# Last group's scatters in one row ahead of all stores, no fills behind the stores, and two more root batches on VectorE

## The chip, the cores and the metric

The kernel runs on one core of one Trainium2 chip. The metric is the device time of one execution in microseconds (us); lower is better. The engines are TensorE (PE), ScalarE (ACT), VectorE (DVE), GpSimd (POOL) and SyncE (SP), which issues plain DMAs. GpSimd issues the indirect DMAs.

## The reference

The input is x, 4 x 1024 rows of 128 float32. Two stages follow each other, each with a residual and a layer norm.

```python
x = _layernorm(x + _L0_attn_ref(x, ...), axis=-1)    # linear attention, 16 heads of 8, 32 features each
x = _layernorm(x + _L0_ffn_ref(x, ...), axis=-1)
# _layernorm: (x - mean) / sqrt(var + 1e-05)
# _L0_ffn_ref:
scores = jnp.einsum('bsh,he->bse', x, wr) + br
expert_id = jnp.argmax(scores, axis=-1)
h = jax.nn.gelu(jnp.einsum('bsh,ehf->ebsf', x, w1) + b1[:, None, None, :], approximate=False)
y = jnp.einsum('ebsf,efh->ebsh', h, w2) + b2[:, None, None, :]
out = jnp.einsum('ebsh,bse->bsh', y, one_hot)        # every row keeps the one of 8 experts that it chose
```

## The kernel before, in words

**Attention.** The 4096 rows are 32 tiles of 128 rows, in 8 groups of four (G = 8, GT = 4). Keys and values come first, then, group by group, queries, attention, output projection, residual and layer norm. ScalarE writes the normalised rows of a group into `x1`, and VectorE works out for each row its expert and its row number `dest` in a DRAM buffer `sorted_rows` in which the rows lie by expert.

**Scatter.** `scatter(g, tiles)` on GpSimd writes tiles of 128 rows of group g to their places in `sorted_rows`, one indirect DMA each (the issuing line is L553). Each row takes its token number along.

**Experts.** NT = 39 tiles of 128 sorted rows run through the FFN of their expert, tile t in step t. SP loads the rows of a tile (`load_rows`) and its first weight (`load_weights`). A sorted tile may be loaded only once the rows in it have been scattered: tiles 0 to 8 wait for groups 0 to 3, tiles 9 to 16 for groups 0 to 5, and tiles from NB = 17 on for all eight groups (L456). On TensorE, step s transposes tile s + 2 (L821), multiplies tile s + 1 by the first weight (`up`, L828), and tile s by the second (`down`, L841). ScalarE applies GELU (L1004). `down(t)` needs the output bank of tile t - 4, so `add_row(t - 4)` must be done.

**VectorE's step.** `tile_step(s)` adds the product of tile s to its rows (`add_row`, L1334), adds the bias of tile s + 1 (`add_bias`, L1328), takes mean and variance of tile s (L1338, L1342), and normalises the tiles that the table `NORMALISED_IN` lists for step s (`normalise_tile`, L1378). For the normalisation it needs 1/sqrt(var + eps), and that comes in one of three ways. Tiles in `BATCHES` get it from a power on GpSimd (`inverse_deviations`, L570), for which VectorE first adds epsilon (`add_row_epsilon`, L1348). Tiles in `ROOTS` get it from 12 small VectorE instructions (`root`, L1359 to L1369): a first guess from the bits of the number and three Newton steps, four instructions in each of the three steps after the last tile of the batch. Tiles 37 and 38 get it from ScalarE's logarithm and exponential and three VectorE instructions (L1622 to L1633).

**Store.** `store(t)` on GpSimd waits until tile t is normalised and writes its rows to the output by token number, one indirect DMA (L581). SP waits for all 39 stores at the end.

**GpSimd's order** is written out by hand. It takes its queue in program order. Behind the scatters of the last three groups and behind the stores of tiles 0 to 31 stands `keep_apart()`: a fill of `apart`, 128 x 408 float32, that nothing reads (L576), and that waits for the fill before it. `POWER_BEFORE` says ahead of which store a power stands. At the end of the attention part the order is:

```python
scatter(G - 2, range(GT))
inverse_deviations(0)
for t in range(GT):
    scatter(G - 1, (t,))
    store(t)
for t in range(GT, NT):
    if t in POWER_BEFORE:
        inverse_deviations(POWER_BEFORE[t])
    store(t)
```

Of the kernel before, what the change touches and what calls it, by code (L numbers as in the profile page):

```python
# [22 lines left out]
I32 = mybir.dt.int32  # L23
# [10 lines left out]
def build(nc, x, w_qkv, proj, w_out, b_out, wr, br, w1, b1, w2, b2, out):  # L34
# [24 lines left out]
    with ctx:  # L59
# [290 lines left out]
        def rank_slots(g):  # L350
# [10 lines left out]
        BATCHES = [range(0, 6), range(22, 25), range(25, 28), range(28, 31), range(31, 33), range(33, 35), range(35, 37)]  # L361
        ROOTS = [range(t, t + 4) for t in range(6, 22, 4)]
# [9 lines left out]
        NORMALISED_IN = {s: (s - 6,) for s in range(6, 25)}  # L372
        NORMALISED_IN |= {25: (19, 20), 26: (21, 22), 27: (23,), 28: (24,), 29: (25, 26), 30: (27,), 32: (28, 29), 33: (30,), 34: (31, 32),
                          36: (33, 34)}
        POWER_BEFORE = {19: 1, 24: 2, 28: 3, 29: 4, 32: 5, 34: 6}
# [90 lines left out]
        def _(pool):  # L466
# [78 lines left out]
            def scatter(g, tiles):  # L545
                ring = g % XR
                pool.wait_ge(dest_ready, g + 1)
                pool.wait_ge(number_ready, g + 1)
                if g == 0:
                    pool.wait_ge(prefilled, 16 * NPF)  # L550
                for i in tiles:
                    pool.wait_ge(x1_ready, GT * g + i + 1)
                    g_.indirect_dma_start(out=sorted_rows, out_offset=bass.IndirectOffsetOnAxis(ap=dest[:, ring, i:i + 1], axis=0),  # L553
                                          in_=x1[:, ring, i, :], in_offset=None).then_inc(scattered[ring], 16)
                    if g >= G - 3:
                        keep_apart()
# [22 lines left out]
            def store(t):  # L579
                pool.wait_ge(y_ready, t + 1)  # L580
                g_.indirect_dma_start(out=out_rows, out_offset=bass.IndirectOffsetOnAxis(ap=row_slot(t)[:, D:D + 1].bitcast(I32), axis=0),  # L581
                                      in_=row_slot(t)[:, 0:D], in_offset=None, bounds_check=last_token,
                                      oob_is_err=False).then_inc(stored, 16)
                if t < 32:
                    keep_apart()
# [30 lines left out]
            for t in range(GT):  # L616
                scatter(G - 1, (t,))
                store(t)
            for t in range(GT, NT):
                if t in POWER_BEFORE:  # L620
                    inverse_deviations(POWER_BEFORE[t])
                store(t)
# [425 lines left out]
        def _(dve):  # L1048
# [301 lines left out]
            def root(n, i):  # L1350

                at = slice(ROOTS[n][0], ROOTS[n][-1] + 1)
                first = guess[:, 0, :]
                now = guess[:, (i - 3) // 3 % 2, :]
                better = guess[:, ((i - 3) // 3 + 1) % 2, :] if i < ROOT_STEPS - 1 else rstd3[:, at]
# [4 lines left out]
                elif i == 1:  # L1360
                    op = v.tensor_scalar(bits_half[:, :], ve3[:, at].bitcast(I32), 1, None, ALU.arith_shift_right)
                elif i == 2:
                    op = v.tensor_scalar(first.bitcast(I32), bits_half[:, :], -1.0, float(0x5F3759DF), ALU.mult, ALU.add)
                elif i % 3 == 0:
                    op = v.tensor_tensor(var_guess[:, :], ve3[:, at], now, ALU.mult)
                elif i % 3 == 1:
                    op = v.scalar_tensor_tensor(less_half[:, :], var_guess[:, :], -0.5, now, ALU.mult, ALU.mult)
                else:
                    op = v.scalar_tensor_tensor(better, less_half[:, :], 1.5, now, ALU.add, ALU.mult)  # L1369
# [272 lines left out]
            add_row(NT - 2)  # L1642
            add_bias(NT - 1)
            row_statistics(NT - 2)
            row_moments(NT - 2)
            normalise_tile(last[0])
            normalise_tile(last[1])
            add_row(NT - 1)
# [38 lines left out]
```

## Time and profile before

| | |
|---|---|
| device time, median of 3 runs | 221.98 us (221.76 to 222.09) |
| profiled execution, its own time | 221.01 us |
| profiled execution, span from first to last instruction | 219.3 us |
| TensorE busy | 194.5 us (89% of the span), mean granted clock 0.964 |
| VectorE busy | 161.8 us (74%) |
| ScalarE busy | 145.4 us (66%) |
| GpSimd busy | 142.1 us (65%) |

The shares are means over the span. The attention part takes the first 120 us or so; the expert tiles run from there to the end. The rows further below are read from the trace of the same execution. A row of a timeline gives the start in us, the duration in us, the engine, the line, the operation and, in brackets, the idle time of the engine ahead of it and what ended it.

### The profile page before, as it was taken

Reading aid. Unit: us, or ns where it says so; the run is one execution under the profiler, and the core shown is the slowest. Engines: PE = TensorE matmul, PEld = TensorE weight load, DVE = VectorE, ACT = ScalarE, POOL = GpSimd, SP = SyncE. Lnnn points to the kernel's source line nnn. Section 1 sums busy time; section 2 is a strip of 40 time slices with the busy share of each in tenths; the row PEclk is TensorE's granted clock in tenths of the full one; section 3 lists DMA queues with packets and bytes.
Section 4 is the critical chain, followed back from the end, with each engine's and each line's share of the span. In section 5 each row is a group of like instructions: output and inputs, shape, how many; then the busy total and the mean of one; then the engine's idle time right before and its main releaser. Section 6 shows DMA issues by size and latency. Waiting matters only on the chain.

```text
span 219.3 us, 6084 instructions
## 1 busy us (share of the span) xinstructions
PE 194.5 (89%) x1698; PEld 154.7 (71%) x1698; DVE 161.8 (74%) x607; ACT 145.4 (66%) x379; POOL 142.1 (65%) x202
## 2 busy tenths in 40 slices
PE   7999999999999999999998989999499999999300
PEld 2677888888764565545443979899399999999200
DVE  2477778786755999999999768798938788375561
ACT  3487788888757677787675488785346666666420
POOL 8425142342599024676653787988987879988985
PEclk9999999999999999999999999999969999999855
DMA  4899999999993000110117673786378775750010
GB/s 110 230 369 417 411 408 402 401 400 397 304 273 83 0 1 1 52 37 25 40 52 240 176 217 109 196 232 183 92 229 229 225 210 182 203 149 24 26 36 7
DMA packets 28417, 40.46 MB, mean 184 GB/s; under 512 B 3497, under 2 KB 18126, under 8 KB 28384
## 3 DMA queue, kind: packets, MB, share of 16 engines
q1 hardware_dynamic: 26112, 35.80, 51.2%
q0 software_dynamic: 2272, 4.27, 5.7%
q8 instruction: 15, 0.25, 0.5%
q14 instruction: 18, 0.15, 0.2%
HBM read 17.95 MB, written 22.56 MB: 185 GB/s over the span
## 4 chain that ended last, share of the span: by engine, by line
PE 58%; POOL 21%; DVE 6%; issue 5%; ACT 3%; DMA 3%; another core or an unknown queue 1%; SPq 0%; DVEq 0%; ACTq 0%; POOLq 0%
PE pair L319 19%; POOL out_dram L581 11%; PE bank L675 6%; PE pair L828 6%; POOL apart L576 5%; PE pair L841 4%; PE bank L755 4%; PE pair L778 3%; POOL sorted_rows L553 3%; PE pair L755 3%; POOL rstd L570 3%; PE pair L720 2%; PE pair L645 2%; PE bank L655 2%; PE bank L319 2%
## 5 line engine op out<-in xcount | busy, mean ns | idle before, releaser
L1004 ACT ACTIVATE qfeat<-pair,w_sb 128x128 f32<-128x128 f32 x156 | 44.6, 368 | 21.8 <-issue 11.3
L828 PE MATMUL pair<-xsT,w_slot 128*128 128x128 f32 x312 | 42.3, 280 | 0.6 <-issue 0.2
L553 POOL DMA_INDIRECT sorted_rows<-x,dest x32 | 32.0, 1001 | 13.6 <-issue 6.5
L828 PEld LDWEIGHTS pair<-xsT,w_slot 128*128 128x128 f32 x312 | 38.6, 195 | 1.5 <-issue 1.3
L592 POOL TENSOR_TENSOR ksum<-kfeat 128x512 f32<-128x512 f32 x12 | 16.6, 1380 | 31.1 <-DVE kfeat L1092 31.1
L319 PE MATMUL pair<-wkv_part,xT_all 128*128 128x256 f32 x192 | 34.1, 321 | 1.5 <-ACT vals L927 0.8
L841 PE MATMUL pair<-w_sb,qfeat 128*128 x232 | 31.7, 281 | 0.5 <-DVE res L1149 0.5
L319 PEld LDWEIGHTS pair<-wkv_part,xT_all 128*128 128x128 f32 x192 | 28.5, 188 | 5.0 <-issue 4.9
L581 POOL DMA_INDIRECT out_dram<-x_all x26 | 26.0, 999 | 6.9 <-issue 4.3
L841 PEld LDWEIGHTS pair<-w_sb,qfeat 128*128 128x128 f32 x232 | 29.0, 196 | 0.8 <-issue 0.7
L319 PE MATMUL pair<-xT_all,wq_part 128*128 128x512 f32 x72 | 24.2, 456 | 0.0
L940 ACT ACTIVATE qexp<-pair,minus_one 128x512 f32<-128x512 f32 x24 | 16.5, 688 | 10.2 <-PE pair L319 10.1
L576 POOL MEMSET apart<- 128x408 f32 x44 | 20.8, 472 | 0.0
L1092 DVE SCALAR_TENSOR_TENSOR kfeat<-pair,qexp 128x512 f32<-128x512 f32 x16 | 11.0, 691 | 11.2 <-ACT vals L927 7.5
L534 POOL TENSOR_TENSOR rstd<-var_eps,minus_half 128x4 f32<-128x4 f32 x8 | 8.4, 1049 | 16.3 <-DVE var_eps L1168 16.2
L1121 DVE SCALAR_TENSOR_TENSOR qfeat<-pair,qexp 128x512 f32<-128x512 f32 x24 | 16.3, 683 | 2.4 <-ACT qexp L940 2.3
L1378 DVE TENSOR_SCALAR x_all<-x_all,mv,rstd 128x128 f32<-128x128 f32 x24 | 9.0, 437 | 9.8 <-POOL rstd L570 9.7
L581 POOL DMA_INDIRECT out_dram<-xs x13 | 13.0, 1000 | 3.1 <-issue 1.8
L319 PEld LDWEIGHTS pair<-xT_all,wq_part 128*128 128x128 f32 x72 | 13.9, 193 | 1.6
L994 ACT COPY xsT<-pair 128x128 f32<-128x128 f32 x39 | 10.8, 277 | 6.3 <-PE pair L821 2.7
L917 ACT ACTIVATE qexp<-pair,zero 128x512 f32<-128x512 f32 x16 | 11.0, 689 | 5.0 <-PE pair L319 3.8
L973 ACT ACTIVATE x<-res,shift,rstd 128x128 f32<-128x128 f32 x32 | 14.0, 491 | 0.1
(203 smaller groups left out, 418.4 us busy)
## 6 DMA issues: line engine op xcount, KB each, us to landing
sorted_rows<-pad_rows SPq DMA_DIRECT2D x11, 1584.0 KB, 22.4
w_slot<-in_L_ffn_w_dram SPq DMA_DIRECT2D x39, 256.0 KB
x_all<-in_L_attn_x_dram SPq DMA_DIRECT2D x8, 256.0 KB, 5.0
w_sb<-in_L_ffn_w_dram SPq DMA_DIRECT2D x4, 512.0 KB, 13.8
x_all<-sorted_rows SPq DMA_DIRECT2D x26, 66.0 KB
xs<-sorted_rows SPq DMA_DIRECT2D x13, 66.0 KB
w_sb<-in_L_ffn_b_dram SPq DMA_DIRECT2D x1, 512.0 KB, 7.0
sorted_rows<-x,dest POOLq DMA_INDIRECT x32
```

Source lines behind the costliest of these rows:

```text
L319: last = nc.tensor.matmul(out[:, to], weights[:, w, :], moving[:, m, of], start=(start and w + m == 0), stop=(w == 1))
L553: g_.indirect_dma_start(out=sorted_rows, out_offset=bass.IndirectOffsetOnAxis(ap=dest[:, ring, i:i + 1], axis=0), in_=x1[:, ring, i, :], i ...
L576: g_.memset(apart[:, :], 0.0).then_inc(apart_set, 1)
L581: g_.indirect_dma_start(out=out_rows, out_offset=bass.IndirectOffsetOnAxis(ap=row_slot(t)[:, D:D + 1].bitcast(I32), axis=0), in_=row_slot( ...
L592: g_.tensor_tensor(ksum[:, n % 2, :], kfeat[:, at, :], kfeat[:, at + 1, :], ALU.add).then_inc(ksum_ready, 1)
L755: last = mm(out[heads, :], kv_diag[:, at:at + CD], qfeat[:, g % 2, k, :], start=True, stop=True, skip_group_check=True)
L828: last = mm(h_bank[t % 2][:, k * P:(k + 1) * P], w1_slot[:, t % WB, k * P:(k + 1) * P], xsT[:, t % 2, :], start=True, stop=True)
L841: last = mm(y_bank[t % 4][:, 0:D], hT[:, t % 2, k * P:(k + 1) * P], w2_sb[:, bass.ds(w_at[t] + k * D, D)], start=(k == 0), stop=(k == FC - 1))
L940: a_.activation(qexp[:, (n + 2) % QB, :], q_bank[n % QB][:, :], ACT.Exp, bias=minus_one[:, :]).then_inc(q_exp, 1)
L973: a_.activation(x1[:, g % XR, i, 0:D], res[:, par, i, :], ACT.Identity, bias=shift[:, par, i:i + 1], scale=rstd[:, par, i:i + 1]).then_inc ...
L1004: a_.activation(hT[:, t % 2, k * P:(k + 1) * P], h_bank[t % 2][:, k * P:(k + 1) * P], ACT.Gelu, bias=w2_sb[:, bass.ds(w_at[t] + (FF + D + ...
L1121: v.scalar_tensor_tensor(qfeat[:, g % 2, k, :], q_bank[n % QB][:, :], 1.0, qexp[:, (n + 2) % QB, :], ALU.max, ALU.min).then_inc(q_done, 1)
```

## The change

Five things change.

1. The four scatters of group 7 stand one behind the other, ahead of store 0. Before, store 0 stood behind the first scatter, store 1 behind the second, and so on.
2. No store has a fill behind it (32 fills fewer). Of groups 5 and 6 the last scatter has none either (2 fewer). The scatters of group 7 keep theirs.
3. Tiles 22 to 28 move from GpSimd powers to VectorE roots, as batches 22 to 25 and 26 to 28. `root` works on as many columns as its batch has tiles.
4. Tiles 29 to 36 are powers in three batches (29 to 31, 32 and 33, 34 to 36), ahead of stores 27, 30 and 34. With batch 0 to 5 that makes four powers in the expert part where there were seven.
5. `NORMALISED_IN` follows, and in the step of tile 37 tile 34 is normalised ahead of `add_bias(38)`, tiles 35 and 36 behind the moments of tile 37.

```diff
-        BATCHES = [range(0, 6), range(22, 25), range(25, 28), range(28, 31), range(31, 33), range(33, 35), range(35, 37)]
-        ROOTS = [range(t, t + 4) for t in range(6, 22, 4)]
+        BATCHES = [range(0, 6), range(29, 32), range(32, 34), range(34, 37)]
+        ROOTS = [range(t, t + 4) for t in range(6, 26, 4)] + [range(26, 29)]
...
-        NORMALISED_IN = {s: (s - 6,) for s in range(6, 25)}
-        NORMALISED_IN |= {25: (19, 20), 26: (21, 22), 27: (23,), 28: (24,), 29: (25, 26), 30: (27,), 32: (28, 29), 33: (30,), 34: (31, 32),
-                          36: (33, 34)}
-        POWER_BEFORE = {19: 1, 24: 2, 28: 3, 29: 4, 32: 5, 34: 6}
+        NORMALISED_IN = {s: (s - 6,) for s in range(6, 28)}
+        NORMALISED_IN |= {28: (22, 23), 29: (24,), 30: (25,), 31: (26,), 32: (27, 28), 33: (29, 30), 34: (31,), 35: (32, 33)}
+        POWER_BEFORE = {27: 1, 30: 2, 34: 3}
...
-                    if g >= G - 3:
+                    if g >= G - 3 and (i < GT - 1 or g == G - 1):
                         keep_apart()
...
                                       oob_is_err=False).then_inc(stored, 16)
-                if t < 32:
-                    keep_apart()
...
             inverse_deviations(0)
-            for t in range(GT):
-                scatter(G - 1, (t,))
-                store(t)
-            for t in range(GT, NT):
+            scatter(G - 1, range(GT))
+            for t in range(NT):
                 if t in POWER_BEFORE:
                     inverse_deviations(POWER_BEFORE[t])
                 store(t)
...
             def root(n, i):
-
+                count = len(ROOTS[n])
                 at = slice(ROOTS[n][0], ROOTS[n][-1] + 1)
-                first = guess[:, 0, :]
-                now = guess[:, (i - 3) // 3 % 2, :]
-                better = guess[:, ((i - 3) // 3 + 1) % 2, :] if i < ROOT_STEPS - 1 else rstd3[:, at]
+                first = guess[:, 0, 0:count]
+                now = guess[:, (i - 3) // 3 % 2, 0:count]
+                better = guess[:, ((i - 3) // 3 + 1) % 2, 0:count] if i < ROOT_STEPS - 1 else rstd3[:, at]
...
             last = BATCHES[-1]
             add_row(NT - 2)
+            normalise_tile(last[0])
             add_bias(NT - 1)
             row_statistics(NT - 2)
             row_moments(NT - 2)
-            normalise_tile(last[0])
             normalise_tile(last[1])
+            normalise_tile(last[2])
             add_row(NT - 1)
```

GpSimd's queue around the last group's scatters, before (`sorted_rows` is the target of a scatter, `out_dram` of a store, `apart` of a fill, `rstd` of a power):

```order
L553 DMA sorted_rows<-x,dest 33792x132
L576 MEMSET apart 128x408
L570 TENSOR_TENSOR rstd<-ve,minus_half 128x6
L553 DMA sorted_rows<-x,dest 33792x132
L576 MEMSET apart 128x408
L581 DMA out_dram<-xs 4096x128
L576 MEMSET apart 128x408
L553 DMA sorted_rows<-x,dest 33792x132
L576 MEMSET apart 128x408
L581 DMA out_dram<-xs 4096x128
L576 MEMSET apart 128x408
L553 DMA sorted_rows<-x,dest 33792x132
```

And now, from the same scatter, the fourth of group 6, on (line numbers are one lower in the changed kernel):

```order
L552 DMA sorted_rows<-x,dest 33792x132
L569 TENSOR_TENSOR rstd<-ve,minus_half 128x6
L552 DMA sorted_rows<-x,dest 33792x132
L575 MEMSET apart 128x408
L552 DMA sorted_rows<-x,dest 33792x132
L575 MEMSET apart 128x408
L552 DMA sorted_rows<-x,dest 33792x132
L575 MEMSET apart 128x408
L552 DMA sorted_rows<-x,dest 33792x132
L575 MEMSET apart 128x408
L580 DMA out_dram<-xs 4096x128 x13
L580 DMA out_dram<-x_all 4096x128 x14
```

The fill ahead of the power is gone, the stores that stood between the scatters stand behind the fourth, and 27 stores follow each other with nothing between them.

GpSimd's queue at the end, before, from the power ahead of store 28 on:

```order
L570 TENSOR_TENSOR rstd<-ve,minus_half 128x3
L581 DMA out_dram<-x_all 4096x128
L576 MEMSET apart 128x408
L570 TENSOR_TENSOR rstd<-ve,minus_half 128x2
L581 DMA out_dram<-x_all 4096x128
L576 MEMSET apart 128x408
L581 DMA out_dram<-x_all 4096x128
L576 MEMSET apart 128x408
L581 DMA out_dram<-x_all 4096x128
L576 MEMSET apart 128x408
L570 TENSOR_TENSOR rstd<-ve,minus_half 128x2
L581 DMA out_dram<-x_all 4096x128 x2
L570 TENSOR_TENSOR rstd<-ve,minus_half 128x2
L581 DMA out_dram<-x_all 4096x128 x5
```

And now, the last five rows that issue anything:

```order
L569 TENSOR_TENSOR rstd<-ve,minus_half 128x3
L580 DMA out_dram<-x_all 4096x128 x3
L569 TENSOR_TENSOR rstd<-ve,minus_half 128x2
L580 DMA out_dram<-x_all 4096x128 x4
L569 TENSOR_TENSOR rstd<-ve,minus_half 128x3
L580 DMA out_dram<-x_all 4096x128 x5
```

Before, four powers and four fills stand ahead of or between the stores 28 to 38. Now the three powers shown stand ahead of stores 27, 30 and 34, and no fill is left.

## Rows read from the trace of the kernel before

**Rows 1.** The page's head.

```profile
span 219.3 us, 6084 instructions
```

**Rows 2.** The chain of waits from 150 us on: start us, us, what.

```profile
152.91 2.21 DMA sorted_rows<-x,dest
...
155.88 1.72 DMA x_all<-sorted_rows
...
180.88 0.98 POOL out_dram L581
```

**Rows 3.** Busy us by stretch: PE, PEld, DVE, ACT, POOL, granted clock, DMA share, GB/s.

```profile
157.60:163.60 6.00, 5.74 (x35) 5.58 (x36) 2.49 (x15) 2.23 (x9) 5.37 (x8) 0.72 0.80 220
...
181.00:204.50 23.50, 23.50 (x210) 23.22 (x208) 14.86 (x62) 16.34 (x61) 20.90 (x29) 1.00 0.46 132
```

**Rows 4.** Timeline of TensorE; L841 rows are down of tiles 14, 24, 31 and 38.

```profile
153.77 1.06 PE L841 MATMUL pair<-w_sb,qfeat 128*128 x8
157.65 0.33 PE L821 MATMUL pair<-ident,x_all 128*128 128x128 f32 x1 [2.82 <-DMA x_all<-sorted_rows]
...
177.85 1.06 PE L841 MATMUL pair<-w_sb,qfeat 128*128 x8
...
191.12 1.06 PE L841 MATMUL pair<-w_sb,qfeat 128*128 x8
...
203.35 1.15 PE L841 MATMUL pair<-w_sb,qfeat 128*128 x8
```

**Rows 5.** Timeline of GpSimd; L553 scatters, L581 stores, L570 powers, L576 fills.

```profile
141.07 0.45 POOL L576 MEMSET apart<- 128x408 f32 x1
141.47 1.36 POOL L570 TENSOR_TENSOR rstd<-ve,minus_half 128x6 f32<-128x6 f32 x1
143.03 1.09 POOL L553 DMA_INDIRECT sorted_rows<-x,dest  x1 [0.20 <-issue]
...
146.51 0.97 POOL L553 DMA_INDIRECT sorted_rows<-x,dest  x1 [0.17 <-issue]
...
148.10 1.00 POOL L581 DMA_INDIRECT out_dram<-xs  x1 [0.17 <-issue]
...
182.24 0.95 POOL L570 TENSOR_TENSOR rstd<-ve,minus_half 128x3 f32<-128x3 f32 x1
...
210.59 0.74 POOL L570 TENSOR_TENSOR rstd<-ve,minus_half 128x2 f32<-128x2 f32 x1
211.51 1.04 POOL L581 DMA_INDIRECT out_dram<-x_all  x1 [0.18 <-issue]
212.86 0.98 POOL L581 DMA_INDIRECT out_dram<-x_all  x1 [0.30 <-issue]
...
216.71 0.98 POOL L581 DMA_INDIRECT out_dram<-x_all  x1 [0.30 <-issue]
```

**Rows 6.** Timeline of ScalarE, the last tile of group 7.

```profile
145.66 0.51 ACT L973 ACTIVATE x<-res,shift,rstd 128x128 f32<-128x128 f32 x1
```

**Rows 7.** Who waited for whom on SP's queue, 118 us to the end.

```profile
SPq L456 <- DMA sorted_rows<-x,dest: 5.3, 1, 5.3
```

**Rows 8.** Timeline of VectorE: a normalisation, then `add_row` of tiles 10, 11 and 14.

```profile
146.74 0.76 DVE L1378 TENSOR_SCALAR xs<-xs,mv,rstd 128x128 f32<-128x128 f32 x1
...
150.14 0.29 DVE L1334 TENSOR_TENSOR xs<-pair,xs 128x128 f32<-128x128 f32 x1 [0.17 <-issue]
...
152.19 0.29 DVE L1334 TENSOR_TENSOR xs<-pair,xs 128x128 f32<-128x128 f32 x1
...
156.43 0.29 DVE L1334 TENSOR_TENSOR x_all<-pair,x_all 128x128 f32<-128x128 f32 x1
```

**Rows 9.** Timeline of all engines, the normalisation of tile 38.

```profile
214.37 0.34 DVE L1639 TENSOR_SCALAR x_all<-x_all,mv,rstd 128x128 f32<-128x128 f32 x1
```

**Rows 10.** The normalisations by tile of `x_all`: duration ns min/median/max, first and last start.

```profile
L1378 DVE TENSOR_SCALAR x_all<-x_all,mv,rstd x24: 315/346/891, 170.7 to 211.7; 128x128 f32<-128x128 f32 x24
```

**Rows 11.** Who waited for whom, 180 us to the end: us, times, longest.

```profile
DVE x_all L1378 <- POOL rstd L570: 9.7, 4, 2.9
```

More of the change, by code:

```diff
@@ L1350, in root @@
             def root(n, i):
+                count = len(ROOTS[n])
                 at = slice(ROOTS[n][0], ROOTS[n][-1] + 1)
-                first = guess[:, 0, :]
-                now = guess[:, (i - 3) // 3 % 2, :]
-                better = guess[:, ((i - 3) // 3 + 1) % 2, :] if i < ROOT_STEPS - 1 else rstd3[:, at]
+                first = guess[:, 0, 0:count]
+                now = guess[:, (i - 3) // 3 % 2, 0:count]
+                better = guess[:, ((i - 3) // 3 + 1) % 2, 0:count] if i < ROOT_STEPS - 1 else rstd3[:, at]
+                halved, scaled_guess, less = bits_half[:, 0:count], var_guess[:, 0:count], less_half[:, 0:count]
                 reach(dve, guess_step, ROOT_STEPS * n + i)
@@ L1360, in root @@
                 elif i == 1:
-                    op = v.tensor_scalar(bits_half[:, :], ve3[:, at].bitcast(I32), 1, None, ALU.arith_shift_right)
+                    op = v.tensor_scalar(halved, ve3[:, at].bitcast(I32), 1, None, ALU.arith_shift_right)
                 elif i == 2:
-                    op = v.tensor_scalar(first.bitcast(I32), bits_half[:, :], -1.0, float(0x5F3759DF), ALU.mult, ALU.add)
+                    op = v.tensor_scalar(first.bitcast(I32), halved, -1.0, float(0x5F3759DF), ALU.mult, ALU.add)
                 elif i % 3 == 0:
-                    op = v.tensor_tensor(var_guess[:, :], ve3[:, at], now, ALU.mult)
+                    op = v.tensor_tensor(scaled_guess, ve3[:, at], now, ALU.mult)
                 elif i % 3 == 1:
-                    op = v.scalar_tensor_tensor(less_half[:, :], var_guess[:, :], -0.5, now, ALU.mult, ALU.mult)
+                    op = v.scalar_tensor_tensor(less, scaled_guess, -0.5, now, ALU.mult, ALU.mult)
                 else:
-                    op = v.scalar_tensor_tensor(better, less_half[:, :], 1.5, now, ALU.add, ALU.mult)
+                    op = v.scalar_tensor_tensor(better, less, 1.5, now, ALU.add, ALU.mult)
                 op.then_inc(guess_step, 1)
```

## The prediction

> **What bounds the kernel now.** I read the page's head first, then the chain of waits, then the timelines of the engines on it. The head gives the span, 219.3 us [rows 1]. From 150 us on the chain has three parts. First the last scatter of group 7 and the load of tile 17's rows behind it [rows 2]. Then TensorE, tile after tile. Then, from 180.88, GpSimd's stores to the end [rows 2]. So two things can be gained, and they lie one behind the other.
>
> The first is a hole on TensorE. It starts `down(14)` at 153.77 and then stands idle for 2.82 us until the rows of tile 17 have come, at 157.65 [rows 4]. The hole costs more than its length, because the granted clock is 0.72 in the six microseconds behind it, where it is 1.00 from 181 us on [rows 3]. The pitch of a tile gives the whole price. From tile 24 to tile 31 TensorE takes 191.12 - 177.85 = 13.27 us, 1.896 us a tile. From tile 14 to tile 24 it takes 177.85 - 153.77 = 24.08 us, where ten tiles at that pitch are 18.96 [rows 4]. The hole costs 5.12 us.
>
> The second is GpSimd's queue at the end. From 181 us on it is busy for 20.90 of 23.50 us [rows 3]. TensorE starts its last `down` at 203.35 [rows 4], yet the last store starts at 216.71, and the last stores run without a gap that anything but their own issue explains [rows 5]. The last tile is normalised from 214.37 on [rows 9], 2.3 us before its store. VectorE waits here for GpSimd's powers, 9.7 us in four waits [rows 11]. The bound of the last 36 us is therefore the number of things in GpSimd's queue.
>
> **The scatters.** GpSimd's power for tiles 0 to 5 starts at 141.47 behind a fill that starts at 141.07 [rows 5]. Without that fill it can start 0.40 earlier, and the first scatter of group 7 starts at 143.03 - 0.40 = 142.63. From there each step is a scatter and a fill. A store with a fill takes what a scatter with a fill takes, so I read the pitch from the mixed row. Two pitches behind a power are 146.51 - 143.03 = 3.48, the third 148.10 - 146.51 = 1.59 [rows 5]. The fourth scatter starts at 142.63 + 3.48 + 1.59 = 147.70, not at 152.91 [rows 2]. Its data are there, since ScalarE ends that tile at 145.66 + 0.51 = 146.17 [rows 6].
>
> From the start of that scatter to tile 17 on TensorE it took 157.65 - 152.91 = 4.74 us: 2.21 for the scatter to land, SP's issue, 1.72 for the load [rows 2, 4]. Now the rows are there at 147.70 + 4.74 = 152.44. TensorE wants them at 157.65 - 2.82 = 154.83 [rows 4]. That leaves 2.4 us. SP is not late either: its 5.3 us wait for the scatters [rows 7] ended at 155.1, so it began at 149.8, and the scatter now lands at 147.70 + 2.21 = 149.9. I take the whole hole as gone, **5.12 us** on TensorE. The last `down` starts at 198.23. The first fill removed, behind group 5, is worth nothing, since the next scatter waits for VectorE's row numbers.
>
> **The stores.** Store 0 moves back from behind the first scatter to 147.70 + 1.59 = 149.3. Nobody waits for a store but SP at the very end, so that is free as long as GpSimd catches up. It does. Stores without a fill follow each other at (216.71 - 212.86) / 3 = 1.28 us [rows 5], and tiles come every 1.90. The queue that has built up is gone near store 11, at about 163. From there GpSimd waits for VectorE, which runs six tiles behind TensorE, until the catching up begins.
>
> I start the sum of the tail at store 26. Its tile is normalised in step 31, with four root instructions and one epsilon. The same mix stood in step 24, whose store, number 18, started at 180.88, and that is 3.03 us after `down(24)` at 177.85 [rows 2, 4]. `down(31)` now starts at 191.12 - 5.12 = 186.00, so store 26 starts at 189.03. Behind it stand twelve stores and three powers, nothing else:
> - a power of two columns: the store ahead takes 0.98, the power and the gap to the next store 211.51 - 210.59 = 0.92 [rows 5], together 1.90
> - a power of three columns is longer by 0.95 - 0.74 = 0.21 [rows 5], so 2.11. There are two of these and one of the above
> - the store behind a power takes 212.86 - 211.51 = 1.35 to the next [rows 5], three times
> - six more pitches of 1.28
>
> That is 1.90 + 4.22 + 4.05 + 7.70 = 17.87 us. Store 38 starts at **206.90 instead of 216.71**. Of the 9.81 us, 5.12 are the hole and 4.7 come from fills and powers that are gone.
>
> The data must be there in time. The power for tiles 34 to 36 ends near 201.5 in this sum. Before, the last power ended at 210.59 + 0.74 = 211.33 and the last normalisation started 3.04 us later [rows 5, 9]. Now an `add_bias`, one pair of statistics and one more normalisation stand in between, about 1.1 us by their rows' lengths. So tile 38 is normalised from 205.7 on and ready 1.2 us before its store.
>
> **The roots.** 24 small instructions come to VectorE in steps 26 to 31. When VectorE was behind and ran on its own, three steps with four root instructions took 156.43 - 152.19 = 4.24, or 1.41 each, and a step in which a batch begins took 152.19 - 150.14 = 2.05 [rows 8]. TensorE's pitch is 1.90. Two such steps with 2.05 and four with 1.41 to 1.7 (two tiles normalised) fit under it. Cost 0, bounds 0 and 0.5 us; the cover is the 0.2 to 0.5 us that a step has left over. If it fails, store 26 is late by as much.
>
> What the longer steps contain is a wait. A normalisation takes 0.346 us at the median and up to 0.891 [rows 10]. The one of 0.76 at 146.74 ends at 147.50 [rows 8], just as the scatter that GpSimd started at 146.51 ends, at 147.48 [rows 5]. The Trainium skill ("SBUF — State Buffer", Who interferes with whom) says that GpSimd shares one pair of ports with VectorE's two-port operations, that the one that starts first has it for its whole instruction, and that the other is fully blocked. The trace agrees in that one direction: the stretching is on VectorE. By itself the rule speaks against packing the stores, and it is the last rival.
>
> **The total.** The span becomes 219.3 - 9.8 = 209.5. The profiled execution took 221.01 us, 1.71 more than its span, and lies 0.97 below the median of 221.98. I subtract from the median: 221.98 - 9.8 = **212.2 us**.
>
> **The rivals.**
> - *The stores do not get closer.* While TensorE and the loads are busy, a store without a fill might still keep the pitch of 1.59, so that the fills only stood in time that was lost anyway. For it: the rows with 1.28 are all from the end, where little else runs. Against it: it is a gap on GpSimd's own queue. Twelve pitches of 0.31 are 3.7 us, giving 215.9. Chance 0.08.
> - *The hole stays, or another takes its place.* Tile 17's rows, or a weight, might be late behind stores that are now denser, or VectorE's lag (its `add_row(14)` starts at 156.43, `down(14)` ends at 153.77 + 1.06 = 154.83 [rows 4, 8], so 1.6 us) might reach TensorE. Whole hole: 217.3; half of it: 214.8. The spare of 2.4 us speaks against it. Chance 0.10.
> - *Slower: VectorE loses its turns.* With a fill there is a second gap per store in which a blocked VectorE instruction gets its turn. Without it, VectorE might have to wait one more store, 1.28 us, in each step. Its step would be 1.41 + 1.28 = 2.69 us instead of 1.90. Between tile 17 and store 26 lie 14 steps, so store 26 would come 11.1 us later and the kernel would take 223.3. It decides from 0.70 us more per step, since 9.8 / 14 = 0.70. Against it: then GpSimd has to wait for VectorE, is idle, and the blocking ends by itself; it only lasts while a queue of ready tiles is left. Chance 0.06, with all other mishaps on that side.
>
> **How the numbers follow.** My case has a chance of 0.75. Its own bounds are 0.5 for the roots, 0.4 for the first scatters' phase, 0.5 for the end of VectorE's chain, and about 1 us for a power that is asked for earlier or later than I think, to either side: 210.8 to 213.8. The range reaches up to take in the first rival and most of the second: 210.6 to 216.2. About 0.2% is what a measurement of this kernel can tell. All cases but the last and a little of what I have not thought of are faster by more: 0.91 faster, 0.02 the same, 0.07 slower.
>
> **What would show it.** In the profile of the changed kernel I expect the fourth scatter of group 7 near 147.7, no idle time of TensorE behind `down(14)` and a granted clock of 1.00 there, `down(38)` starting near 198.2, stores 1.28 us apart from store 26 on, and the last near 206.9. The step on the hole is wrong if TensorE still waits for rows at tile 17. The step on the stores is wrong if their pitch in the stretch from 189 us on is not 1.28. The step on the roots is wrong if VectorE's steps 26 to 31 last longer than 1.9 us and TensorE or GpSimd waits for them. A wait of VectorE for the power ahead of tile 34 is expected and costs nothing.

## The result and the profile after

The changed kernel takes **224.93 us** (224.37 to 225.76, four runs), the kernel before 222.03 beside it: a ratio of 1.0129, 95% interval 1.0094 to 1.0164. It is slower by 1.3%, where 212.2 us and a gain of 9.8 were forecast. The profiled execution took 225.76 us.

The head of the page of the changed kernel (busy us and share by engine, then TensorE's granted clock in 40 slices), which answers to [rows 1]:

```profile
span 224.0 us, 6060 instructions
...
PE 196.3 (88%) x1691; PEld 155.7 (69%) x1698; DVE 158.2 (71%) x628; ACT 145.5 (65%) x379; POOL 123.9 (55%) x165
...
PEclk9999999999999999999999999999589999999975
```

No engine is busier than 88%, and the clock has a dip near 160 us, as before. GpSimd's timeline of the changed kernel, which answers to [rows 5] (L552 scatters, L575 fills, L580 stores):

```profile
148.11 0.96 POOL L552 DMA_INDIRECT sorted_rows<-x,dest  x1 [0.42 <-ACT x L968]
149.07 0.45 POOL L575 MEMSET apart<- 128x408 f32 x1
149.69 1.00 POOL L580 DMA_INDIRECT out_dram<-xs  x1 [0.17 <-issue]
150.99 0.99 POOL L580 DMA_INDIRECT out_dram<-xs  x1 [0.30 <-issue]
...
156.21 0.98 POOL L580 DMA_INDIRECT out_dram<-xs  x1 [0.33 <-issue]
160.39 0.98 POOL L580 DMA_INDIRECT out_dram<-xs  x1 [3.20 <-DVE xs L1374]
...
221.46 0.98 POOL L580 DMA_INDIRECT out_dram<-x_all  x1 [0.31 <-issue]
```

GpSimd does what was forecast up to 157 us: the fourth scatter at 148.11 (forecast 147.7), the stores 1.29 us apart. Then it waits 3.20 us for rows, and its last store starts at 221.46 instead of 206.90. The rows are late because TensorE is. Its timeline (L816 turn, L823 up, L836 down; the downs shown are those of tiles 12, 13, 14 and 36 to 38), for [rows 4]:

```profile
151.65 1.06 PE L836 MATMUL pair<-w_sb,qfeat 128*128 x8
154.48 0.30 PE L816 MATMUL pair<-ident,x_all 128*128 128x128 f32 x1 [1.78 <-issue]
154.97 1.13 PE L823 MATMUL pair<-xsT,w_slot 128*128 128x128 f32 x8 [0.18 <-issue]
159.22 2.07 PE L836 MATMUL bank<-w_sb,qfeat 128*128 x8 [3.13 <-ACT qfeat L999]
...
161.30 1.91 PE L823 MATMUL pair<-xsT,w_slot 128*128 128x128 f32 x8
163.00 1.74 PE L836 MATMUL pair<-w_sb,qfeat 128*128 x8
...
208.14 1.16 PE L836 MATMUL pair<-w_sb,qfeat 128*128 x8 [0.28 <-issue]
...
211.24 1.16 PE L836 MATMUL bank<-w_sb,qfeat 128*128 x8 [1.01 <-issue]
214.28 1.15 PE L836 MATMUL pair<-w_sb,qfeat 128*128 x8 [1.89 <-ACT qfeat L999]
```

No row waits for tile 17's load any more. Instead `down(13)` is 7.57 us behind `down(12)`, where 1.90 is the pitch, and from it on three groups of eight run in 1.7 to 2.1 us instead of 1.06. What TensorE waited for is seen on ScalarE, in its timeline (L989 the copy of the turned rows, L999 the gelu):

```profile
150.11 1.14 ACT L999 ACTIVATE qfeat<-pair,w_sb 128x128 f32<-128x128 f32 x4 [0.60 <-issue]
154.07 0.27 ACT L989 COPY xsT<-pair 128x128 f32<-128x128 f32 x1 [2.83 <-remote]
158.61 1.14 ACT L999 ACTIVATE qfeat<-pair,w_sb 128x128 f32<-128x128 f32 x4 [4.27 <-remote]
```

The copy needs the turn ahead of `down(12)`, which ended at 150.92, yet starts at 154.07; the gelu needs an up that ended at 156.10 (154.97 + 1.13) at the latest, yet starts at 158.61. Both waits are put down to "remote", a release that the profile finds at no engine of this core. The chain of waits of the changed kernel has such pieces too (start, us), and it comes to GpSimd only at 214.70, with the last power, where it stood there from 180.88 on before [rows 2]:

```profile
151.25 2.81 another core or an unknown queue
154.36 4.08 another core or an unknown queue
...
195.51 2.02 another core or an unknown queue
```

VectorE waits at the same moments, at each `add_row` for a down:

```profile
154.46 0.29 DVE L1329 TENSOR_TENSOR xs<-pair,xs 128x128 f32<-128x128 f32 x1 [3.12 <-PE pair L836]
...
158.62 0.29 DVE L1329 TENSOR_TENSOR xs<-pair,xs 128x128 f32<-128x128 f32 x1 [2.69 <-remote]
```

SP's queue waits too (5.4 us on remote), for an up. All of them wait for TensorE, and the trace shows it directly, since it also holds the time at which a semaphore update arrived (a part of the updates is missing from it). The turn ahead of `down(12)` ended at 150.92, and its update stands at 154.05. `down(12)` ended at 152.71, and its update stands at 158.53, 5.8 us later. From 118 us on, 27 of the 86 recorded updates of TensorE stand over 0.25 us behind the end of their instruction; of the 348 of VectorE, ScalarE and GpSimd none stands over 0.03 us behind. Towards TensorE nothing is late either: ScalarE's copy ends at 154.34 and the turn that waits for it starts at 154.48, while GpSimd issues a store (153.57 to 154.55). So the engines hear late from TensorE, and from nobody else. In the busy time by stretch of the changed kernel (columns of [rows 3]) the engines fall silent together while GpSimd issues its stores:

```profile
154.00:158.00 4.00, 1.43 (x9) 1.11 (x9) 1.47 (x9) 0.27 (x1) 2.56 (x3) 0.95 0.19 61
158.00:162.00 4.00, 2.78 (x13) 2.79 (x14) 2.05 (x12) 2.60 (x10) 0.98 (x1) 0.50 0.44 103
```

The clock of 0.50 (1.2 of 2.4 GHz) comes behind that idle time and makes it dearer. The same happens, shorter, at the next dense stores (193 to 198 and 200 to 212 us), which is where `down(38)` loses the rest.

One such piece stood in the chain of the kernel **before**, behind three scatters without a fill, and the prediction did not read it:

```profile
123.48 1.33 another core or an unknown queue
```

### The profile page after: what moved, and what is told of

It is laid out like the page before. It is cut to its first block, busy times and chain, and to the rows that moved or that the text cites. A ratio compares the mean times of both kernels' runs of the same rounds, so it can differ in the third digit from the quotient of the medians.

```text
span 224.0 us, 6060 instructions
## 1 busy us (share of the span) xinstructions
PE 196.3 (88%) x1691; PEld 155.7 (69%) x1698; DVE 158.2 (71%) x628; ACT 145.5 (65%) x379; POOL 123.9 (55%) x165
## 3 DMA queue, kind: packets, MB, share of 16 engines
q0 software_dynamic: 2272, 4.27, 5.5%
## 4 chain that ended last, share of the span: by engine, by line
PE 66%; DVE 7%; ACT 7%; issue 6%; another core or an unknown queue 5%; DMA 3%; POOL 3%; SPq 1%; ACTq 1%; DVEq 0%
PE pair L319 19%; PE pair L823 11%; PE pair L836 6%; PE bank L670 6%; PE bank L836 4%; PE bank L750 4%; PE pair L773 3%; PE pair L750 3%; ACT qfeat L999 3%; POOL out_dram L580 2%; DMA xs<-sorted_rows 2%; PE pair L715 2%; PE bank L650 2%; PE pair L816 1%
## 5 line engine op out<-in xcount | busy, mean ns | idle before, releaser
L999 ACT ACTIVATE qfeat<-pair,w_sb 128x128 f32<-128x128 f32 x156 | 44.6, 370 | 28.2 <-PE pair L823 9.1
L823 PE MATMUL pair<-xsT,w_slot 128*128 128x128 f32 x312 | 42.6, 281 | 1.1 <-issue 0.5
L823 PEld LDWEIGHTS pair<-xsT,w_slot 128*128 128x128 f32 x312 | 38.7, 195 | 2.3 <-issue 2.1
L552 POOL DMA_INDIRECT sorted_rows<-x,dest x32 | 32.0, 1001 | 14.2 <-issue 6.6
L580 POOL DMA_INDIRECT out_dram<-x_all x26 | 25.7, 989 | 16.7 <-DVE x_all L1374 12.7
L836 PE MATMUL pair<-w_sb,qfeat 128*128 x232 | 31.6, 280 | 2.7 <-ACT qfeat L999 1.9
L836 PEld LDWEIGHTS pair<-w_sb,qfeat 128*128 128x128 f32 x232 | 29.0, 196 | 3.3 <-issue 3.3
L580 POOL DMA_INDIRECT out_dram<-xs x13 | 12.8, 987 | 12.8 <-DVE xs L1374 11.1
L1329 DVE TENSOR_TENSOR x_all<-pair,x_all 128x128 f32<-128x128 f32 x19 | 5.5, 292 | 18.4 <-PE pair L836 11.1
L989 ACT COPY xsT<-pair 128x128 f32<-128x128 f32 x39 | 10.8, 276 | 10.2 <-remote 6.3
L836 PE MATMUL bank<-w_sb,qfeat 128*128 x80 | 11.9, 295 | 4.2 <-ACT qfeat L999 3.1
```

What stands on the lines that cost most here:

```text
L823: last = mm(h_bank[t % 2][:, k * P:(k + 1) * P], w1_slot[:, t % WB, k * P:(k + 1) * P], xsT[:, t % 2, :], start=True, stop=True)
L836: last = mm(y_bank[t % 4][:, 0:D], hT[:, t % 2, k * P:(k + 1) * P], w2_sb[:, bass.ds(w_at[t] + k * D, D)], start=(k == 0), stop=(k == FC - 1))
L999: a_.activation(hT[:, t % 2, k * P:(k + 1) * P], h_bank[t % 2][:, k * P:(k + 1) * P], ACT.Gelu, bias=w2_sb[:, bass.ds(w_at[t] + (FF + D + ...
```

## The experiments

Theory S: while GpSimd issues an indirect DMA (0.98 us), semaphore updates are held. A gap of 0.30 us to the next one is too short to let them through, a fill widens it. The expectations speak of the updates of all other engines; late in any trace are TensorE's alone (VectorE's, ScalarE's and GpSimd's stand at most 0.08 us behind). Its rivals differ from run to run. All ratios are to the kernel before, run beside each on the same chip.

**e1: fills back.** All else of the change stays.

```
  def store(t): ...
+     if t < 32:
+         keep_apart()
```

> The changed kernel with the fills put back behind stores 0 to 31; order of scatters, roots and powers as changed. Theory S (spacing): where GpSimd issues several indirect DMAs with only 0.3 us between them, the semaphore updates of all other engines are held up for 1 to 4 us; the fills prevent that. Then the idle times of TensorE at 152.7 to 154.5, 155.9 to 159.2 and 196.9 to 198.0 us of the changed kernel's profile disappear, the last down starts near 198 us, and the kernel takes 213 to 216 us (the sum of the prediction plus six fills in the tail, about 2 us). Rival P (position): the held-up updates come with the program's position (an instruction fetch, the loads of weights) or with the scatters in a row, whatever the spacing: still 223 to 226 us. Rival R (roots): the 24 added VectorE instructions cost the time: still above 222 us.

218.66 us, ratio 0.9884 (0.9841 to 0.9927): 2.7 us faster than the kernel before beside it, where the change is 2.9 slower. So the fills alone, which cost GpSimd 0.31 us each, give 5.6 us. At the stores no hole of that size is left; but the time is 2.7 us above the range. TensorE and ScalarE of e1 show why (L838 down, L825 up, L1001 gelu):

```profile
158.48 1.13 PE L825 MATMUL pair<-xsT,w_slot 128*128 128x128 f32 x8
159.50 1.16 PE L838 MATMUL pair<-w_sb,qfeat 128*128 x8
...
161.06 1.13 PE L825 MATMUL pair<-xsT,w_slot 128*128 128x128 f32 x8 [0.29 <-issue]
```

```profile
161.34 1.14 ACT L1001 ACTIVATE qfeat<-pair,w_sb 128x128 f32<-128x128 f32 x4 [1.15 <-remote]
```

The up ends at 159.61 and the gelu starts 1.7 us later, where 0.2 us is usual (in e12 below an up ends at 154.83 and its gelu starts at 155.02). There is no hole, but from 152 to 166 us the downs stand 2.3 to 2.5 us apart instead of 1.90. Even with the fill updates of TensorE come up to 1.8 us late (the one at 156.38).

**e2: fills behind the first six stores only** (`if t < 6`).

> The changed kernel with fills behind stores 0 to 5 only, the stores of its first dense stretch (149.7 to 157.2 us). Theory S: the hole of TensorE at 152 to 159 us is gone, and some stalls remain behind dense stretches later (193 to 197 us and from 203 us on); 216 to 220 us. Rival P: no difference from the changed kernel, 224 to 225 us.

221.62 us, ratio 1.0008 (0.9976 to 1.0041), above the range. The stall moved to the first stores without a fill: 1.84 us of issue at 161.6 in the chain, where TensorE's update at 164.22 is 4.1 us late, and 1.94 and 2.25 us of another core at 191.7 and 204.9. So neither the scatters in a row nor the place of the stores makes the stall; it follows the missing fill.

**e3: the kernel before without its fills behind stores.** Nothing else of the change.

> The kernel before with the fills behind its stores taken out and nothing else. If a fill only costs its 0.31 us of GpSimd's queue, 14 fills fewer in the stretch from 181 us on, in which GpSimd is the bound, give 217 to 218 us. Theory S: stalls of TensorE with late semaphore updates appear where stores stand close together (from 154 us on and in the last 30 us), and the kernel takes 222 us or more.

224.48 us, ratio 1.0151 (1.0109 to 1.0193): this one part makes the kernel before as slow as the whole change does.

**e4: the kernel before with the last scatters in a row.**

```
- for t in range(GT):
-     scatter(G - 1, (t,))
-     store(t)
- for t in range(GT, NT):
+ scatter(G - 1, range(GT))
+ for t in range(NT):
```

> The kernel before with the four scatters of group 7 in a row ahead of store 0, all fills kept, nothing else. The prediction's first step alone: the wait for the rows of tile 17 (2.8 us idle and 2.3 us of slow clock, 5.1 us in all) goes, GpSimd's queue of the tail starts as much earlier: 216.5 to 218 us. If TensorE stays idle near tile 17 for another reason: 221 to 223 us.

220.21 us, ratio 0.9949 (0.9914 to 0.9984). The hole at tile 17 is gone, but its 5.12 us are not gained: the downs stand 2.2 to 2.6 us apart from 154 to 166 us, much as in e1, and the last one starts at 201.11 instead of 203.35. e1 differs from this run in the roots and powers (and two fills behind scatters) and is 1.5 us faster, though its last down starts at 203.18: the gain lies in GpSimd's queue behind it.

**e5: fills of half the width** (`apart[:, 0:204]`).

> The changed kernel with a fill of half the width (128x204) behind stores 0 to 31; e1 had the whole width there. The fill of 128x408 makes the pitch of the stores 1.60 us instead of 1.29; half of it should make some 1.4. Theory S (what matters is the gap between two indirect DMAs of GpSimd, in which the other engines' semaphore updates get through): the dose counts, so the stalls are between those of the changed kernel and of e1: waits on 'remote' of 1 to 2 us at the first six stores instead of 2.7 to 4.3, time 216 to 222. If the stalls are gone as in e1, GpSimd's queue is shorter by 0.15 us a store behind the hold-up, and the time is 214 to 216. Rival F (the fill itself, a write of GpSimd with a semaphore update, lets the others through, however short it is): no stalls, 214 to 216.

223.04 us, ratio 1.0094 (1.0068 to 1.012). The pitch is 1.43. From `down(12)` to `down(15)` it takes 13.20 us, where the change takes 13.94 and e1 6.60: the stall is between the two, but close to the change's. GpSimd and the chain of e5:

```profile
153.68 0.98 POOL L580 DMA_INDIRECT out_dram<-xs  x1 [0.16 <-issue]
...
155.11 0.98 POOL L580 DMA_INDIRECT out_dram<-xs  x1 [0.16 <-issue]
```

```profile
156.38 1.66 another core or an unknown queue
```

The time is above the range given, too, nearer to the change than to e1. That a fill helps however short it is (rival F) is out.

**e6: waits as spacing.** Eight waits on semaphores long reached behind each store, no fill.

> The changed kernel with eight waits of GpSimd on semaphores that have long been reached behind each of stores 0 to 31, no fill: time passes on GpSimd's sequencer and nothing is written. How long eight such waits take no row shows; the waits on this engine's sequencer that stand in the trace take some 0.05 us each, so the pitch should be near 1.6. Theory S: if the pitch is 1.5 or more, no stalls at the first six stores, and the time is that of e1, 217 to 220. Rival F: the stalls stay as in the changed kernel (2.7 to 4.3 us on 'remote'), 223 to 226, whatever the pitch is. If the pitch stays under 1.4, the run tells nothing between the two.

223.17 us, ratio 1.012 (1.0055 to 1.0185). The pitch stayed at 1.29: the waits cost nothing, and the stall stayed too (ScalarE waits 5.64 us on remote at 156.28). So the run tells nothing between spacing and the fill's own effect.

**e7: two fills behind each of stores 0 to 11**, one behind 12 to 31.

> e1 (fills behind stores 0 to 31) with a second fill behind each of stores 0 to 11, so their pitch is about 2.1 us instead of 1.60. In e1 TensorE's down groups stand 2.3 to 2.5 us apart from 152 to 166 us instead of 1.90, without a stall of over 0.3. Theory S: what is left of the held updates does this (the last matmul of an up group ends and the gelu starts 1.5 to 2 us later instead of 0.2); with the wider gap the down groups stand 1.90 to 2.0 apart, TensorE ends its last down 2 to 3 us earlier than in e1 (200 to 201.5 instead of 203.2), but GpSimd, which is never idle for long from 149 us on in e1, ends 12 x 0.5 = 6 us later or, where it makes it up while it waits for rows from 165 to 187, 0 to 3 us later: time 218 to 224. Rival T (the 2.4 us are ScalarE's or TensorE's own, from row loads or VectorE's roots): the spacing of the downs stays 2.3 to 2.5.

221.75 us, ratio 1.002 (0.9992 to 1.0048). With a pitch of 2.09 TensorE runs freely where e1 did not (L840 down):

```profile
150.38 1.06 PE L840 MATMUL pair<-w_sb,qfeat 128*128 x8
...
152.28 1.06 PE L840 MATMUL bank<-w_sb,qfeat 128*128 x8
...
154.17 1.06 PE L840 MATMUL pair<-w_sb,qfeat 128*128 x8
...
156.26 1.06 PE L840 MATMUL pair<-w_sb,qfeat 128*128 x8
```

The rival T falls. But as GpSimd makes up its queue with a pitch of 1.60 from 174 us on, ScalarE waits 1 us on remote twice more (180.2, 189.8), and TensorE starts its last down at 202.86, not at 200 to 201.5 as expected.

**e8: stores that write one row.** The bound of the row numbers at 0 leaves out every row of the output but row 0.

```
- last_token = pool.to_reg(B * N - 1)
+ last_token = pool.to_reg(0)
```

> The changed kernel with the bound of the stores' row numbers at 0, so that all rows but row 0 of the output are left out: the stores are issued as before, but write nothing (the output is left unwritten but for one row). No fills. Theory G (GpSimd's issue of an indirect DMA, the making of its descriptors, holds the updates): the issue still takes 0.98 us at a pitch of 1.29, the stalls at the first six stores are the same, 2.7 to 4.3 us, and the time is 222 to 226. Rival W (the writes and completions of the stores' 128 rows hold them): stalls gone, the time 212 to 216.

222.36 us, ratio 1.0056 (1.0022 to 1.0089). GpSimd and the chain of e8:

```profile
154.40 0.98 POOL L580 DMA_INDIRECT out_dram<-xs  x1 [0.31 <-issue]
155.69 0.98 POOL L580 DMA_INDIRECT out_dram<-xs  x1 [0.30 <-issue]
159.73 0.98 POOL L580 DMA_INDIRECT out_dram<-xs  x1 [3.06 <-DVE xs L1374]
```

```profile
154.86 3.05 another core or an unknown queue
194.21 1.94 another core or an unknown queue
```

Issue, pitch and stall are as in the change though next to nothing is written (GpSimd's DMA queue moves 2.19 MB in the whole run instead of 4.27, and the scatters are in both). What comes with the issue of the indirect DMA makes TensorE's updates late, not its writes.

**e9, e10, e11.** These three shared a chip. e9 has fills in one partition (`apart[0:1, :]`, pitch 1.57). e10 is e1 with `if t < 32 and t + 1 not in POWER_BEFORE`. e11 is e10 with fills from group 4 on (`g >= G - 4`).

> The changed kernel with a fill of 1x408 instead of 128x408 behind stores 0 to 31: as many elements in a row and so, if a fill's duration goes by them, the same spacing as in e1 (1.60 us), with 1/128 of what is written. Theory S (only the spacing of the indirect DMAs counts): as e1, no stall of over 0.5 us on TensorE at the first six stores, 217 to 220. Rival F (what the fill writes, in all partitions, is what lets the others through): the stalls of the changed kernel, 2.7 to 4.3 us, and 223 to 226. If the fill is shorter and the pitch 1.4, as with the half fills, 221 to 224 under S.

> e1 (fills behind stores 0 to 31) without the fill where a power follows (stores 26 and 29; behind 33 e1 has none already), so that the power of 0.9 us is the spacing. If GpSimd's queue bounds the end of e1 (it is never idle for over 0.7 us from 187.5 us to the last store), it ends 2 x 0.31 to 2 x 0.47 us earlier, and no new stall comes: 217.6 to 218.2. If it is TensorE that bounds it (last down at 203.2 in e1), no change, 218.4 to 218.9.

> e10 with fills behind the scatters of group 4 too, which both the kernel before and the changed one issue without (120.7, 122.2 and 123.5 us in e1, with ScalarE's xsT copy late by 1.35 us on 'remote' and 1.34 us of 'another core or an unknown queue' in the chain at 123.7). Theory S, at a place that the change does not touch: that stall and that row of the chain go, TensorE is 0.7 to 1.2 us earlier from 125 us on; the scatters end 0.9 us later on GpSimd, which then waits for rows anyway (126.8, 1.12 us). Time: 216.8 to 217.8 if the gain reaches the end; at least not slower than e10 by over 0.3. Rival P (the stall at 124 us comes from elsewhere, TensorE's own order there): the row stays, and the time is 0 to 0.5 us above e10.

They took 213.84 us (ratio 0.9723, 0.9671 to 0.9776), 214.27 (0.9741, 0.9696 to 0.9787) and 214.27 (0.973, 0.9685 to 0.9776). All three are far below every range: e10 is 4.4 us faster than e1 for two fills less. And in none of them has the chain a piece of another core, or any engine a wait on remote, or TensorE an update over 0.04 us late, not even in e9 and e10 behind the unfilled scatters at 120 to 124 us. The kernel before was faster there too, 219.64 us instead of 221.2 to 222.0. That pointed away from the kernels, to the chip.

**e12, e13: the change itself again, and e10's kernel, on one chip.**

> The changed kernel itself once more, next to e10's again on the same chip. In e9, e10 and e11, which ran on one chip, no semaphore update is late anywhere, not even at the three unfilled scatters at 120 to 124 us that have a row of 1.3 us of 'another core or an unknown queue' in the chain of every run before them, on other chips; the kernel before ran 1.6 us faster there too. Theory C (whether a dense row of GpSimd's indirect DMAs holds up the updates is a matter of the chip it runs on; the fills matter only on a chip that does it): on a chip that does it, 223 to 226 again, with two to three rows of 'another core' in the chain; on one that does not, no such row, and 211 to 213.5, near the prediction. Rival K (it is a matter of the kernel: the two fills less in e10, the single partition in e9, took it away): 223 to 226 on any chip, while e10 stays at 214.

> The kernel of e10 again, beside the changed kernel on one chip. Theory C: where the changed kernel shows held updates, this one gives 217.5 to 218.5 with down groups 2.3 to 2.5 us apart at 152 to 166 us, as e1; where it shows none, 214 again, 1.5 to 2.5 us slower than the changed kernel, since its fills only cost GpSimd's time. Rival K: 214 on any chip.

e12, the very kernel that took 224.93 us, took **212.41 us** (211.53 to 212.99), ratio 0.9647 (0.9607 to 0.9687). e13 took 214.05, ratio 0.9727. Theory C holds. TensorE of e12, tiles 13, 14 and 38:

```profile
152.77 1.06 PE L836 MATMUL bank<-w_sb,qfeat 128*128 x8
...
154.66 1.06 PE L836 MATMUL pair<-w_sb,qfeat 128*128 x8
...
199.12 1.16 PE L836 MATMUL pair<-w_sb,qfeat 128*128 x8
```

GpSimd of e12:

```profile
147.34 0.97 POOL L552 DMA_INDIRECT sorted_rows<-x,dest  x1 [0.23 <-ACT x L968]
...
148.92 1.00 POOL L580 DMA_INDIRECT out_dram<-xs  x1 [0.16 <-issue]
150.22 0.99 POOL L580 DMA_INDIRECT out_dram<-xs  x1 [0.31 <-issue]
...
201.46 0.90 POOL L569 TENSOR_TENSOR rstd<-ve,minus_half 128x3 f32<-128x3 f32 x1
...
208.24 0.98 POOL L580 DMA_INDIRECT out_dram<-x_all  x1 [0.30 <-issue]
```

And its busy time where the change fell silent:

```profile
154.00:158.00 4.00, 4.00 (x38) 4.00 (x37) 3.08 (x17) 2.81 (x13) 2.99 (x4) 1.00 0.79 221
```

**e14 to e17: four kernels side by side on another chip**: the change, the kernel before, e10's kernel, e3's kernel.

> The changed kernel a third time, with three kernels beside it on one chip. Theory C (the hold-up of semaphore updates belongs to the chip): on a chip of the first sort (held updates) 222 to 226, on one of the second 211 to 213.5, and the other three kernels of this call go with it. No value between.

> The kernel before, unchanged, to see its trace on the same chip as the change's. On a chip of the first sort as the trace of before: the row of 1.3 us of another core at 123.5 us, a span of 218 to 220. On one of the second sort: no such row at 123.5 us, the hole on TensorE at the load of tile 17's rows stays (the scatter is as late, so down(14) and down(15) are 5 us apart), span 216 to 219.

> e10's kernel (fills behind stores 0 to 31 but not in front of a power). Chip of the first sort: 217.5 to 219, so 4 to 7 us faster than the changed kernel beside it; of the second sort: 213 to 215, 1.5 to 2.5 us slower than the changed kernel beside it.

> The kernel before without the fills behind its stores (e3's kernel), the scatters of the last group still among them. Chip of the first sort: 223 to 225, as e3, 1.5 % slower than before. Second sort: the fills only cost GpSimd 0.31 us each, so 1 to 4 us faster than before on the same chip.

They took 224.76 (ratio 1.0122, 1.0062 to 1.0183), 222.19 (0.9997), 219.84 (0.9894, 0.9829 to 0.996) and 224.49 us (1.0144, 1.0071 to 1.0218; single runs from 222.67 to 226.74): the first sort of chip for all four, as expected, with e10's kernel 0.8 us above its range. The chain of e14:

```profile
154.76 1.66 another core or an unknown queue
194.07 2.02 another core or an unknown queue
```

e10's kernel is 4.9 us faster than the change here and 1.6 us slower in e13. **e18**, the kernel before for its trace on the second sort, met a chip of the first:

> The kernel before, once more, for its trace on a chip of the second sort, if this is one (on one of the first sort it repeats e15: a row of another core near 123.5 us and 221 to 223 us, and tells nothing new). On one of the second sort: no row of another core in the chain, about 219.5 to 220.5 us, the hole on TensorE at tile 17's rows is there (downs 5 us apart near 154), and the last down is at 201 to 203 us; so the 7.8 us between it and the changed kernel's 212.4 are the hole (some 4 to 5), and the tail.

220.88 us, ratio 0.9981 (0.9953 to 1.0009); the hole at tile 17 as in [rows 4]. The chain has no piece of another core here, but updates of TensorE are up to 1.34 us late.

What each chip gave (median us; the change and e10's kernel where they ran; in the last column, of TensorE's recorded updates from 118 us on, those over 0.25 us late, in the trace with the fewest and the one with the most):

| chip | runs | before | change | e10's kernel | updates late |
|---|---|---|---|---|---|
| of the result | - | 222.03 | 224.93 | | 12 of 85 (before), 27 of 86 (change) |
| A | e1 to e4 | 221.36 | | | 27 of 93 to 36 of 94 |
| B | e5 to e8 | 221.15 | | | 21 of 89 to 36 of 89 |
| C | e9 to e11 | 219.64 | | 214.27 | none of 355 in three traces |
| D | e12, e13 | 220.24 | 212.41 | 214.05 | none of 237 in two traces |
| E | e14 to e17 | 222.14 | 224.76 | 219.84 | 14 of 85 (before) to 37 of 97 |
| F | e18 | 220.92 | | | 9 of 82 (before) |

## Why the prediction was wrong

**The step that failed** is the one on the stores: it costs a fill at its 0.31 us on GpSimd's queue, and lets twelve stores, and the queue before them, run 1.28 us apart as if no other engine were touched by it. That put a term at nothing: what denser issues do to TensorE's semaphore updates. On the chip of the result they make them up to 5.8 us late, and the kernel slower by 2.9 us instead of faster by 9.8; the fills had kept that small. The chain of waits held the warning, 1.33 us of another core behind three scatters without a fill at 120 to 124 us, and the prediction passed over it because the row names no engine.

Point by point:
- *The scatters.* Right. The fourth came at 148.11 (e12: 147.34), forecast 147.70, and no run with the scatters in a row waits for tile 17's rows. In e12 the whole hole is gone, and `down(38)` starts at 199.12, forecast 198.23. Where updates come late another hole, and the low clock behind it, took its place: against e12 the change is 0.8 us behind at tile 12 (151.65 - 150.87), 8.3 at tile 14 (163.00 - 154.66), 15.2 at tile 38 (214.28 - 199.12).
- *The stores.* The pitch is right, 1.29 us on both sorts of chip. So the rival that the stores do not get closer is out. What the denser stores do to TensorE's updates was left out. The changed kernel takes 12.5 us more where they come late (224.93 - 212.41); the kernel before differs by 1.8 between the same two chips. The fills of e1 get 5.6 us back.
- *The tail.* In e12 the power for tiles 34 to 36 starts at 201.46, and the last store at 208.24, forecast 206.90. Of the 1.3 us, 0.9 are the later `down(38)`.
- *The roots.* No run tests them alone. In e12 nothing shows them on TensorE: the downs keep their pitch of 1.90 from tile 19 to tile 36. e1 against e4 puts roots, powers and their order, with two fills, at 1.5 us in favour.
- *The total.* 212.2 forecast, 212.41 in e12, 224.93 in the result. The working comes close on the second sort of chip: most of its steps are met there. That the total is met within 0.2 us is luck in part. It was subtracted from the kernel before on the first sort; on the second the gain is 7.8 us against the kernel before beside it (220.24), not 9.8, and that kernel is 1.8 us faster than the 222.03 of the result. Why it is faster was not seen; there is no trace of it from such a chip.
- *The rivals.* The last had the right side and the right trigger, too few gaps between stores, but the wrong victim. It charged VectorE's turns at a shared port and a step of 2.69 us; in fact VectorE's normalisations average 0.35 us from 170 us on both in the change and in e12. What is late is TensorE's signals, and ScalarE, VectorE and SP wait for them, and TensorE then for ScalarE. "Another hole takes its place" had 0.10, but from data that come late, at 217.3 at most.

What stays open:
- What in GpSimd's issue makes TensorE's updates late. That they pass in the gap between two issues is not shown: the updates of the change at 154.05 arrive in the middle of an issue (153.57 to 154.55), those at 158.44 to 158.66 only 1.3 to 1.5 us behind the end of the last one (157.19). And the ends of matmuls in a trace are modelled, so a late end of the work itself would look the same.
- Whether the hold-up belongs to the chip or to something on it that lasted for as long as its runs did, since none of the six was met twice. The traces from the chips with late updates also hold fewer recorded updates of all engines, 2675 to 3004 against 4423 to 4479 on the other two; whether the two have a common cause, or the recording has a part in it, no run tells.
- Why the fill lets updates through, by its spacing or by itself (e6 and e9 were to tell, but e6 made no gap and e9 met the second sort). e7 and e5 move spacing and the amount of filling together.
- Whether fills at group 4 help on the first sort (e11 met the second).

## What to carry to other kernels

An instruction that does nothing, behind every indirect DMA of GpSimd, may be there for the sake of another engine, here TensorE. Before taking it out, look in the chain and the waits for "remote" or "another core" at the places that lack it already; in a kernel of one core they stood for updates of TensorE that came late. A gain or a loss of this sort has to be timed on several chips: here one and the same edit makes the kernel 1.2 to 1.3% slower or 3.5% faster, and e10's version, 1.1% and 2.6 to 2.7% faster than before, is the one of the two timed on both that wins on both.

## What was not expected of the hardware

- While GpSimd issued indirect DMAs with 0.30 us between them, TensorE's semaphore updates arrived up to 5.8 us late on the chip of the result (up to 6.7 in e6), and late on four of the six chips that the experiments met; on the other two never by over 0.04 us. VectorE's, ScalarE's and GpSimd's were late on none. The issue itself takes 0.98 us on all.
- Stores that wrote one row held them up as much as stores that wrote all (a piece of 3.05 us in the chain of e8).
- At 0.61 us between issues updates were still up to 1.8 us late in a dense row (e1); at 1.1 us (e7, stores 0 to 11) only two at the start were, by 0.6 to 0.7 us.
- Eight waits on semaphores already reached took no time that the timeline shows between two stores (e6: pitch 1.29 with and without).
